# Four graph layers on one core: the last stage counts ranks in PSUM, with 0/1 masks per pair and two row blocks by turns

## The reference

```python
support = input @ weight                       # 8192 x 64
mask = (adj != 0)
rank = cumsum(mask, axis=1)                    # running count along each row
deg = rank[:, -1:]
k = minimum(deg, 100)
pos = rank - (deg - k)
w = mask * where(pos > 0, 0.5 ** (k - pos), 0.0)
out = w @ support + bias
```

## Time and profile before

| | |
|---|---|
| median of 3 runs | 2971.34 us |
| profiled execution, its own time | 2968.38 us |
| its span | 2966.6 us |
| PE busy | 2865.3 us, 97% |
| DVE busy | 1994.5 us, 67% |
| ACT busy | 1622.5 us, 55% |
| DMA traffic | 1148.10 MB, 387 GB/s on the mean |
| the last stage | from about 2238 us to the end |

### The profile page before, as it was taken

How to read it: one execution, slowest core, us unless ns; L and a number is a source line. 1 busy time by engine, 2 the same in 40 slices (tenths; PEclk the granted TensorE clock), 3 DMA queues, 4 the chain that set the end, 5 groups by cost and what they waited for, 6 DMA issues and landing times.

```text
span 2966.6 us, 34147 instructions
## 1 busy us (share of the span) xinstructions
PE 2865.3 (97%) x13488; PEld 1815.2 (61%) x13488; DVE 1994.5 (67%) x2033; ACT 1622.5 (55%) x1215; POOL 13.2 (0%) x31
## 2 busy tenths in 40 slices
PE   7999999999999999999999999999888999999998
PEld 3456576775578874788846888554334555555554
DVE  2125356765588875788847988532117999999997
ACT  1125354653467653567725776311006888888887
POOL 0000000000000000000000000000000000000000
PEclk9999999999999999999999999999999999999999
DMA  9999999999999999999999999999999999999995
GB/s 353 417 410 379 404 378 382 376 397 380 407 403 378 369 386 414 397 383 378 377 408 391 385 377 376 399 420 420 421 421 393 375 383 388 387 386 383 376 389 236
DMA packets 158926, 1148.10 MB, mean 387 GB/s; under 512 B 18017, under 2 KB 18257, under 8 KB 19505
## 3 DMA queue, kind: packets, MB, share of 16 engines
q1 hardware_dynamic: 157312, 1143.02, 96.6%
q0 software_dynamic: 1088, 2.48, 0.2%
q10 hardware_dynamic: 368, 0.43, 0.0%
HBM read 1143.75 MB, written 2.10 MB: 386 GB/s over the span
## 4 chain that ended last, share of the span: by engine, by line
PE 79%; DMA 16%; DVE 2%; ACT 1%; issue 1%; SPq 0%; ACTq 0%; DVEq 0%
PE ACC L968 26%; DMA raw<-in_at 16%; PE ACC L1097 15%; PE ACC L975 13%; PE ACC L956 11%; PE PSF L1111 4%; PE PST L1111 4%; DVE lo L670 2%; PE PSF L1077 1%; ACT hi L486 1%; PE PSF L1055 1%; PE PSF L1052 1%; PE PST L991 1%; PE PSF L1059 1%; PE PSF L1050 0%
## 5 line engine op out<-in xcount | busy, mean ns | idle before, releaser
L670 DVE TENSOR_TENSOR lo<-raw,hi 128x2048 fp32r<-128x2048 f32 x448 | 1018.3, 2289 | 328.7 <-ACT hi L486 326.8
L486 ACT CAST hi<-raw 128x2048 fp32r<-128x2048 f32 x448 | 856.7, 1913 | 513.3 <-DMA raw<-in_at 277.4
L968 PE MATMUL ACC<-hi,T 128*128 128x512 f32 x3584 | 894.2, 392 | 14.0 <-ACT hi L486 14.0
L968 PEld LDWEIGHTS ACC<-hi,T 128*128 128x128 f32 x3584 | 671.6, 188 | 173.2 <-issue 33.7
L956 PE MATMUL ACC<-raw,XF 128*64 128x512 f32 x2816 | 651.2, 600 | 54.6 <-DMA raw<-in_at 52.8
L685 DVE SCALAR_TENSOR_TENSOR M<-raw,M 128x512 bf16<-128x512 f32 x1008 | 637.8, 688 | 41.8 <-PE ACC L1097 24.7
L492 ACT ACTIVATE Wf<-ACC,w_bias 128x1024 fp32r<-128x1024 f32 x512 | 568.1, 1114 | 131.9 <-PE ACC L1097 131.3
L1097 PE MATMUL ACC<-M,rank_b 128*128 128x512 bf16 x2032 | 529.6, 383 | 10.2 <-ACT Wf L492 6.7
L975 PE MATMUL ACC<-lo,T 128*128 128x512 f32 x1792 | 483.3, 392 | 6.0 <-DVE lo L670 5.4
L956 PEld LDWEIGHTS ACC<-raw,XF 128*64 128x64 f32 x2816 | 206.1, 137 | 434.6 <-issue 293.3
L975 PEld LDWEIGHTS ACC<-lo,T 128*128 128x128 f32 x1792 | 335.9, 188 | 83.3 <-DVE lo L670 14.4
(11 more groups left out here) (165 smaller groups left out, 1019.7 us busy)
## 6 DMA issues: line engine op xcount, KB each, us to landing
raw<-in_at SPq DMA_DIRECT2D x1088, 1024.0 KB, 7.1
SV<-in_x_cols SPq DMA_DIRECT2D x8, 256.0 KB, 16.7
out<-O POOLq DMA_DIRECT2D x7, 256.0 KB, 6.4
out<-O ACTq DMA_DIRECT2D x1, 256.0 KB, 2.0
w_sb<-in_w POOLq DMA_DIRECT2D x3, 64.0 KB, 8.5
bias<-in_bias_rows ACTq DMA_DIRECT2D x1, 128.0 KB, 9.7
l1w_sb<-in_l_w POOLq DMA_DIRECT2D x2, 64.0 KB, 7.6
rank_f<-in_rank_mats POOLq DMA_DIRECT2D x1, 128.0 KB, 9.3
```

The costliest lines, as they stand in the source:

```text
L486: nc.scalar.copy(hi[:, n % NH], raw[:, c % NR]).then_inc(hi_done, 1)
L670: tt(lo[:, c % NR], raw[:, c % NR], hi[:, n % NH].bitcast(f32), ALU.subtract).then_inc(lo_done, 1)
L968: ins = mm(acc[:, part], w, hi[:, n % NH, s, part], start=p.opens and s == 0 and i == 0, stop=False)
```

## The change

`count` becomes `mask(m)`, once for a pair: one compare of 2 x 1024 columns to 0/1 values in a ring of NM = 6 pairs, which lies in the place of `hi`. One semaphore `mask_done` takes the place of the two `half`; SP's loads wait for it.

The running count is kept in the rank bank: only the first unit of a row clears it (`start=u.o == 0`); each later one adds matrix 1 times the mask of the chunk before and then matrix 0 times its own mask. So a rank bank belongs to one row block (or one half of one) until its end. To keep two banks at work, the rows are taken by turns: first row block 0, its two halves of 512 columns alternating; then row blocks (1, 2), (3, 4), (5, 6), alternating chunk by chunk; then row block 7 in two halves. `units` lists this order: a unit is one rank group, one Exp and one weigh group. In row blocks 0 and 7 a unit has 512 columns (two rank matmuls, one weigh matmul; one and one for the first), in the others 1024 as before.

`evacuate_out(I)` and `rows_out(I)` are no longer placed by pair but two and three units behind the row's last one. OT gets a second buffer, and so do the squares of the outputs (`squared`). The other steps of a row's end are placed anew by the pair with which the row ends (`gone_on`); for rows taken together they follow each other. `out_var`, `out_root` and `out_scale` lie some 4 to 7 pairs later in row block 7.

The core of the diff:

```diff
@@ -88,17 +90,19 @@
     lo, _ = place("lo", [P, NR, 2, BLK], f32r, raw_at)
-    hi, _ = place("hi", [P, NH, 2, BLK], f32r)
+    hi, hi_at = place("hi", [P, NH, 2, BLK], f32r)
     UT, UT_at = place("UT", [P, BLK], f32)
     TT, _ = place("TT", [D, BLK], f32, UT_at)
-    OT, _ = place("OT", [P, BLK], f32, UT_at)
+    OT0, _ = place("OT0", [P, BLK], f32, UT_at)
     ST1, GS_at = place("ST1", [P, Q, 2, D], f32)
     TX, _ = place("TX", [D + 1, BLK], f32, GS_at)
+    OTs = (OT0, place("OT1", [P, BLK], f32, GS_at)[0])
     hT, hT_at = place("hT", [P, HC, BLK], f32)
     xo, _ = place("xo", [P, Q, D], f32, hT_at + 8 * Q * D)
+    squared = (xo, sq)
     l1w_sb, _ = place("l1w_sb", [P, 4, D], f32, hT_at)
...
@@ -132,7 +136,8 @@
     block_bytes = Q * 4 * D * 4
-    M, _ = place("M", [P, Q, BLK], bf16, T_at + 6 * block_bytes)
+    M, _ = place("M", [P, NM, 2, BLK], bf16, hi_at)
+    assert 2 * NM <= 4 * NH
     Wf, _ = place("Wf", [P, NW, BLK], f32r, T_at + 4 * block_bytes)
...
@@ -212,7 +217,33 @@
     n_all = n_pairs + NB * NB * NP
-    n_chunks = NB * G
+
+
+    per_row = NB * NP
+    last_pairs, units, ends_at = [], [], {}
+    for rows in [(0,)] + [(I, I + 1) for I in range(1, NB - 1, 2)] + [(NB - 1,)]:
+        for o in range(per_row):
+            first = len(last_pairs)
+            last_pairs += [(I, NB * NP - 1 - o) for I in rows]
+            for s in range(2):
+                for h in range(2):
+                    I = rows[h % len(rows)]
+                    part = slice(h * HALF, (h + 1) * HALF) if len(rows) == 1 else slice(0, BLK)
+                    chunk = 2 * o + s
+                    before = (first + h % len(rows), 1) if s else (first + h % len(rows) - len(rows), 0)
+                    units.append(Unit(len(units), I, chunk, part, first + h % len(rows), before if chunk else None))
+                    ends_at[I] = units[-1].n
+    n_units = len(units)
+    rank_of_mask, steps_after = {}, {}
+    for u in units:
+        rank_of_mask[u.pair] = u.n
+        if u.before:
+            rank_of_mask[u.before[0]] = max(u.n, rank_of_mask[u.before[0]])
+    for m in range(len(last_pairs)):
+        steps_after.setdefault(max(u.n for u in units if u.pair == m), []).append(m)
+    gone_on = {I: max(m for m, (row, _) in enumerate(last_pairs) if row == I) + 1 for I in range(NB)}
+    for I in range(1, NB - 1, 2):
+        gone_on[I] = gone_on[I + 1]
     last_acc = acc_of[group_order[-1]]
...
@@ -344,19 +375,17 @@
     for I in range(NB - 1):
-        c = n_pairs + (I + 1) * NP * NB - 1
-        due("DVE", c - 2, "out_z", 6, I)
-        due("ACT", c + 2, "ot", 6, I)
-        due("PE", c + 4, "rows", 6, I)
-        due("DVE", c + 8, "out_a", 6, I)
-        due("ACT", c + 6, "out_sq", 6, I)
-        due("DVE", c + 10, "out_d", 6, I)
-
-    c = n_pairs + (NB - 1) * NP * NB - 1
-    due("DVE", c + 11, "out_var", 6, NB - 1)
-    due("ACT", c + 9, "out_root", 6, NB - 1)
+        c, second = n_pairs + gone_on[I], I and I % 2 == 0
+        due("DVE", c - (3 if I == 0 else 18 if second else 20), "out_z", 6, I)
+        due("DVE", c + 2, "out_a", 6, I)
+        due("ACT", c + (8 if second else 4), "out_sq", 6, I)
+        due("DVE", c + (13 if second else 9), "out_d", 6, I)
+
+    c = n_pairs + gone_on[NB - 2]
+    due("DVE", c + 15, "out_var", 6, NB - 1)
+    due("ACT", c + 16, "out_root", 6, NB - 1)
     for I in range(NB - 1):
-        due("DVE", c + 14 + 2 * I, "out_scale", 6, I)
+        due("DVE", c + 18 + 2 * I, "out_scale", 6, I)
     due("DVE", n_all - 2, "out_z", 6, NB - 1)
...
@@ -427,14 +456,13 @@
                 else:
-                    I, o = divmod(c - n_pairs, NB * NP)
-                    J, pr = divmod(NB * NP - 1 - o, NP)
+                    I, at_right = last_pairs[c - n_pairs]
+                    J, pr = divmod(at_right, NP)
                 s, before = c % NR, c - NR
                 elif before >= n_pairs:
-                    sp.wait_ge(half[0], 2 * (before - n_pairs) + 2)
-                    sp.wait_ge(half[1], 2 * (before - n_pairs) + 2)
+                    sp.wait_ge(mask_done, before - n_pairs + 1)
                 sp.dma_start(raw[:, s], at[(I * NB + J) * NP + pr].rearrange(
...
@@ -485,11 +513,12 @@
 
-            def weights(m):
-                act.wait_ge(rank_done, m + 1)
-                if m >= NW:
-                    act.wait_ge(weigh_done, m - NW + 1)
-                nc.scalar.activation(Wf[:, m % NW, :], rank_banks[m % 2], ACT.Exp, scale=-LN2,
+            def weights(u):
+                act.wait_ge(rank_done, u.n + 1)
+                if u.n >= NW:
+                    act.wait_ge(weigh_done, u.n - NW + 1)
+                width = u.part.stop - u.part.start
+                nc.scalar.activation(Wf[:, u.n % NW, 0:width], rank_banks[u.n % 2][:, 0:width], ACT.Exp, scale=-LN2,
                                      bias=w_bias[:, 0:1]).then_inc(wt_done, 1)
...
@@ -503,8 +532,10 @@
             def evacuate_out(I):
-                act.wait_ge(weigh_done, (I + 1) * G)
-                nc.scalar.copy(OT[:], out_acc[I % 2]).then_inc(ot_done, 1)
+                act.wait_ge(weigh_done, ends_at[I] + 1)
+                if I >= 2:
+                    act.wait_ge(rows_done, I - 1)
+                nc.scalar.copy(OTs[I % 2][:], out_acc[I % 2]).then_inc(ot_done, 1)
 
...
@@ -669,21 +702,14 @@
 
-            def count(m):
-                c = n_pairs + m // 2
-                if m % 2 == 0:
-                    dve.wait_ge(raw_in[c % NR], 16 * (c // NR + 1))
-                if m >= Q - 1:
-                    dve.wait_ge(rank_done, m - Q + 2)
-                for h in range(2):
-                    part = slice(h * HALF, (h + 1) * HALF)
-                    src = raw[:, c % NR, 1 - m % 2, part]
-                    if m % G == 0:
-                        ins = ts(M[:, (m + 1) % Q, part], src, 0.0, None, ALU.not_equal)
-                    else:
-                        dve.wait_ge(half[h], m)
-                        ins = stt(M[:, (m + 1) % Q, part], src, 0.0, M[:, m % Q, part], ALU.not_equal, ALU.add)
-                    ins.then_inc(half[h], 1)
+            def mask(m):
+                c = n_pairs + m
+                if m == 0:
+                    dve.wait_ge(hi_used, len(split_no))
+                dve.wait_ge(raw_in[c % NR], 16 * (c // NR + 1))
+                if m >= NM:
+                    dve.wait_ge(rank_done, rank_of_mask[m - NM] + 1)
+                ts(M[:, m % NM], raw[:, c % NR], 0.0, None, ALU.not_equal).then_inc(mask_done, 1)
 
...
@@ -1081,40 +1106,39 @@
                     transpose(PST, O[:, gs(I), :]).then_inc(tpx_done, 1)
-                elif what == "rows":
-                    rows_out(r)
-
-            def rank(m):
-                pe.wait_ge(half[0], m + 1)
-                pe.wait_ge(half[1], m + 1)
-                if m >= 2:
-                    pe.wait_ge(wt_done, m - 1)
-                terms = [(0, (m + 1) % Q, h) for h in range(2)]
-                if m % G:
-                    terms += [(1, m % Q, h) for h in range(2)]
-                for i, (mat, slot, h) in enumerate(terms):
-                    part = slice(h * HALF, (h + 1) * HALF)
-                    ins = mm(rank_banks[m % 2][:, part], rank_b[:, mat, :], M[:, slot, part], start=i < 2,
-                             stop=i >= len(terms) - 2)
+
+            def rank(u):
+                bank, width = rank_banks[u.n % 2], u.part.stop - u.part.start
+                pe.wait_ge(mask_done, u.pair + 1)
+                if u.n >= 2:
+                    pe.wait_ge(wt_done, u.n - 1)
+                terms = [(0, u.pair, 1 - u.o % 2)]
+                if u.before:
+                    terms = [(1, *u.before)] + terms
+                for i, (mat, pair, s) in enumerate(terms):
+                    for h in range(width // HALF):
+                        out_part = slice(h * HALF, (h + 1) * HALF)
+                        part = slice(u.part.start + h * HALF, u.part.start + (h + 1) * HALF)
+                        ins = mm(bank[:, out_part], rank_b[:, mat, :], M[:, pair % NM, s, part], start=u.o == 0,
+                                 stop=i == len(terms) - 1, skip_group_check=True)
                 ins.then_inc(rank_done, 1)
 
-            def weigh(m):
-                I, o = divmod(m, G)
-                g = G - 1 - o
-                if I == 0 and o % Q == 0:
-                    pe.wait_ge(s_done, o // Q + 1)
-                if o == 0 and I >= 2:
-                    pe.wait_ge(rows_used, I - 1)
-                pe.wait_ge(wt_done, m + 1)
-                for h in range(2):
-                    part = slice(h * HALF, (h + 1) * HALF)
-                    ins = mm(out_acc[I % 2][:, part], S[:, g, :], Wf[:, m % NW, part], start=o == 0, stop=o == G - 1)
+            def weigh(u):
+                if u.I == 0 and u.o % Q == 0:
+                    pe.wait_ge(s_done, u.o // Q + 1)
+                if u.o == 0 and u.I >= 2:
+                    pe.wait_ge(rows_used, u.I - 1)
```

(65 more changed lines are left out.)

1 line of the change is left out of this document (removed).

## The result

The changed kernel takes 2990.91 us (median of 4 runs, 2988.29 to 2991.72) beside 2971.61 us for the kernel before on the same chip: ratio 1.0068, 95% interval 1.0056 to 1.0080. The forecast was 2993. The profiled execution takes 2990.43 us with a span of 2988.6, against 2968.38 and 2966.6: +22.0 us, where the sum gave +22. By the ratio of the medians it is +20.2 us, so the forecast was some 2 us high, and that the profiled executions differ by just the sum is in part chance.

What follows compares the result with a forecast made beforehand. PE was taken as the bound, busy 97% of the span. Terms 16 (half units) + 3 (other ACT work) + 4 (row changes) - 0.7 (start) - 1.2 (end) + 1 (clock) gave +22 us: 2993 median, range 2972 to 3006.

Steps and rivals of the forecast that it cites:

- The bound: Last stage: PE sets the pace; DVE's waits cost some 5 us at most, and DVE's relief was taken as 0.
- rival C: Full units: PE pulls first weight loads ahead, 0.05 us gained each; total -8 us, 2963; chance 0.10.
- The half units: Row blocks 0 and 7: bank cycle 1.46 us, units 0.735 us apart against 0.6725; +16 us (3 to 20).
- the missing Exp: Half units of rows 0 and 7: Exp of 512 columns, without a profile row, taken as 0.70 us.
- Rival B: Half units: Exp lasts 0.60 us, so halves cost 3 us instead of 16; +9 us, 2980; chance 0.13.
- Other ACT work: Rows 0 and 7: roots, relu, squares and copies on ACT cost PE more than before; +3 us (1 to 5).
- the clock: Last stage: more standing of PE, perhaps one more dip of the granted clock; +1 us (0 to 3).
- part hides behind PE's inserted work: Rows 0 and 7: some of the 3.8 us summed for other ACT operations is hidden, leaving 3 us.
- Changes of row: Row ends: PE stalls 1.1 us at joint ends, about 1.1 after row 0, 1.95 before row 7; about +4 (0 to 9).
- Rival D: Three row changes: DVE's second add keeps masks back, 3 to 5 us each; +35 to +45, 3010; chance 0.05.
- What would show it: Profile after: DVE about 55%, PE near 97, full units 1.345 us apart, half units 0.735, 1.1 us PE gap at joint row ends.
- ACT Exp as releaser of a PE wait each time: Rows 0 and 7: the profile would name Exp as ending a PE wait at rank groups of two matmuls, 0.735 us apart.

Runs made afterwards that it cites:

- experiment 3: The kernel before with a plain compare in place of DVE's compare-and-add, ranks lacking the running count: 2968.06 us, ratio 0.9996.
- experiments 10: The changed kernel with a linear activation, bias vector kept, in place of Exp in the half units: 2983.04 us, ratio 1.0045.
- experiment 11: The changed kernel with Exp in the half units without the bias vector and with another scale: 2980.53 us, ratio 1.0037.
- experiment 7: The changed kernel with the three roots of its last stage worked out on DVE instead of ACT: 2979.74 us, ratio 1.0037 to the kernel before.

## Why the prediction was right, point by point

**The bound.** PE bound the stage before and after, and a relief of DVE alone is worth nothing: experiment 3 shows it, within 0.1%. The full units kept their 1.345 us, so rival C (fewer waits let the first weight load be pulled ahead) fell: from three counters to two, "issue" still stands before the loads.

**The half units.** The reckoning by the cycle of one bank held: 0.59 + 0.03 + 0.69 + 0.14 = 1.45, measured 1.46. The value for the missing Exp (0.70 for 0.688) was found by adding the difference at 1024 columns to the copy of 512; the reason given ("tables and bias") was half wrong, since the function costs nothing (experiments 10 and 11). That the sum came out so close is partly luck of that kind: this term was 1.1 too high and the next 2.0 too low. Rival B (0.60) would have been right for an Exp without bias vector: experiment 11 is rival B, at 2980.5 where 2980 stood. The figure of the Trainium skill that was weighed there ("VectorE: DVE Perf Modes", the TRN2 errata) gives 0.57, where 0.597 was measured without a bias vector and 0.688 with it; the measurement decides. Another page of the Trainium skill ("ScalarE: Activation LUTs", the section on what ACT_TABLE_LOAD costs) splits the two: 186 ns plus 0.833 a column, and 93 more for each vector operand. By it 612 and 706 ns are estimates for 512 columns, where 597 and 688 were measured; the step of 93 agrees with the 91 here.

**Other ACT work.** The mechanism was right and the size too low: 3 and 1 for the clock, measured 6.0 by what the other terms leave over. The roots cost 2.84 each in row 0 for 2.24, near the forecast 2.68, relu and square 0.98; the deduction "part hides behind PE's inserted work" was wrong, for the gaps that can be read one by one stand in full (experiment 7: three roots fewer gave 9 to 11 us back, 2.84 x 3 = 8.5 and two dips of the clock). The terms as listed add up to 3.9 and not 3.8. In row 7 the root and its dip of the clock were 0.34 more than before (five half units from 2930.96 in 7.91 us, 4.26 over their pace; three full ones from 2891.09 in 7.95, 3.92 over) and had been put at 0.44. The stage has one dip of the clock more than before, as forecast, but at its start and not behind a root.

**Changes of row.** The stall was 1.42 us for 0.42 at (1,2) into (3,4), twice, 1.26 for 0.21 after row 0 and 1.74 for 0.42 before row 7; forecast 1.1, 1.1 and 1.95. Rival D did not come: the masks were ready each time.

**What would show it.** DVE at 56% (55 named), PE at 96, the OT copy as releaser at a joint row end: as written. One sign was wrong: "ACT Exp as releaser of a PE wait each time". In half units the wait is 0.05 to 0.09 us more idle time of a weight load that lags 0.26 anyway, put down to "issue" or to the mask. Someone who had looked for the named releaser alone would have taken DVE for the cause.

## What to carry to other kernels

Halving a unit halves the work but not the fixed costs in the cycle of its buffer: before cutting, add up the cycle of one bank, and look for what in it can be dropped, as here an operand of 0.09 us that is paid in each of 256 units. An engine at 67% on the mean may have 0.2 us a pair to spare in one stage and half its time in another; whether an extra step is cheap there is read from the stage, and the same edit can win 9 to 11 us in one version and 0 to 4 in the other. And an engine's relief is worth what it lets happen next; here that was nothing until the roots moved onto it.

## What the runs showed of the hardware

- A bias vector costs an activation from PSUM 0.09 us at 512 columns (687 for 597 ns), the function nothing; at 1024 columns Exp with it takes 1115 ns, the copy without it 1006, and no run parts function and bias there.
- One compare of 2048 columns takes 1226 ns, four of 512 would take 4 x 424 = 1696: an estimate of 0.16 us for each call more.
- DVE operations on 8 columns take 0.17 us each, 0.20 apart when each awaits the last, and a wait for its own last operation costs DVE 0.23 us.
- The first weight load of a rank group lags 0.26 to 0.28 us where nothing is late, under "issue" or under the name of an engine long done (174 times in row blocks 1 to 6); a short wait for Exp shows as 0.32 to 0.35 in its place, under the same names.
